# A tile stage written out for 71 tiles, with the routing weight made in the tile from the difference of two logits

## The reference

```python
logits = einsum('bth,he->bte', z, rW) + rb
probs = softmax(logits);  topv, topi = top_k(probs, 2)
mask = sum(one_hot(topi, 8) * topv[..., None], axis=-2)
w = mask / maximum(sum(mask, -1), 1e-8)
hid = gelu(einsum('bth,ehf->btef', z, W1) + b1)          # exact gelu, W1: 8 x 256 x 512
outs = einsum('btef,efh->bteh', hid, W2) + b2            # W2: 8 x 512 x 256
mixed = sum(outs * w[..., None], axis=2);  return x + mixed
```

## Time and profile before

| | |
|---|---|
| median of 3 runs | 596.23 us (595.38 to 596.32) |
| the profiled execution | 598.88 us, of which its span (first to last instruction) 597.0 us |
| granted TensorE clock, mean | 0.937 of full speed |
| busy: PE, PEld, DVE, ACT, POOL | 477.8, 395.3, 443.5, 350.3, 338.7 us |
| tile stage, first hb to last hb | 285.30 to 551.68 us |
| DMA | 69.95 MB in 50125 packets, 10160 of them under 512 B |

### The profile page before, as it was taken

How to read it: one execution, slowest core, us unless ns; L and a number is a source line. 1 busy time by engine, 2 the same in 40 slices (tenths; PEclk the granted TensorE clock), 3 DMA queues, 4 the chain that set the end, 5 groups by cost and what they waited for, 6 DMA issues and landing times.

```text
span 597.0 us, 13147 instructions
## 1 busy us (share of the span) xinstructions
PE 477.8 (80%) x2775; PEld 395.3 (66%) x2776; DVE 443.5 (74%) x1469; ACT 350.3 (59%) x788; POOL 338.7 (57%) x266
## 2 busy tenths in 40 slices
PE   0388899889999885795999999999999999999300
PEld 0138888777888773542797788798887888887200
DVE  6999786999889848347677777777767777777283
ACT  6992845475676567613465565565655565565365
POOL 0000567643778874660367667767666676666547
PEclk9998999989999986988999999999999999999855
DMA  6205700131335669724435444444444443443497
GB/s 183 101 1 205 289 1 1 59 137 47 131 126 168 199 199 326 238 100 126 152 66 79 67 67 72 71 70 71 64 68 71 71 68 65 70 64 51 61 402 284
DMA packets 50125, 69.95 MB, mean 117 GB/s; under 512 B 10160, under 2 KB 39728, under 8 KB 49584
## 3 DMA queue, kind: packets, MB, share of 16 engines
q1 hardware_dynamic: 34528, 51.81, 26.2%
q0 software_dynamic: 15568, 17.81, 17.9%
HBM read 37.90 MB, written 31.69 MB: 117 GB/s over the span
## 4 chain that ended last, share of the span: by engine, by line
PE 45%; DVE 21%; issue 11%; ACT 10%; POOL 5%; DMA 3%; SPq 3%; another core or an unknown queue 1%; POOLq 0%; DVEq 0%; ACTq 0%
PE psum L1436 14%; PE psum L1455 13%; PE psum L1445 5%; PE psum L1330 3%; PE psum L1423 3%; POOL acc L1254 3%; DVE st L702 2%; PE psum L1301 2%; DVE ws L896 2%; SPq L394 1%; PE psum L1288 1%; DMA y_rows<-yw,dst 1%; POOL y_rows L1231 1%; ACT dump L593 1%; PE psum L1350 1%
## 5 line engine op out<-in xcount | busy, mean ns | idle before, releaser
L1231 POOL DMA_INDIRECT y_rows<-yw,dst x71 | 115.7, 1630 | 66.1 <-issue 22.8
L1436 PE MATMUL psum<-ws,z_hl 128*128 x426 | 119.0, 415 | 3.4 <-DVE z_hl L1094 2.5
L1455 PE MATMUL psum<-ws,h_hl 128*128 x852 | 115.9, 285 | 0.1
L1455 PEld LDWEIGHTS psum<-ws,h_hl 128*128 128x128 f32 x852 | 103.5, 189 | 0.3 <-issue 0.3
L1218 POOL DMA_INDIRECT wt<-w_rows,widx x71 | 70.1, 987 | 44.1 <-issue 18.0
L652 ACT ACTIVATE hg<-hb 128x512 f32<-128x512 f32 x71 | 44.9, 632 | 85.1 <-DVE hb L1102 74.6
L1436 PEld LDWEIGHTS psum<-ws,z_hl 128*128 128x128 f32 x426 | 76.3, 190 | 20.3 <-issue 5.2
L1176 POOL DMA_INDIRECT z_rows<-zn,pos x64 | 68.9, 1076 | 27.2 <-issue 17.1
L1102 DVE TENSOR_TENSOR hb<-psum,b1r 128x512 f32<-128x512 f32 x71 | 49.1, 692 | 36.8 <-issue 34.5
L1330 PE MATMUL psum<-yf,it 128*128 128x256 f32 x256 | 60.9, 395 | 2.6 <-DVE r L945 2.6
L638 ACT ACTIVATE z_f<-psum,gb 128x128 f32<-128x128 f32 x142 | 56.0, 443 | 11.1 <-PE psum L1423 8.9
(11 more groups left out here) (206 smaller groups left out, 854.7 us busy)
## 6 DMA issues: line engine op xcount, KB each, us to landing
z_in<-z_rows SPq DMA_DIRECT2D x71, 129.0 KB
w_raw<-in_dram SPq DMA_DIRECT2D x16, 512.0 KB, 5.9
xs<-in_dram SPq DMA_DIRECT2D x8, 512.0 KB, 5.8
x_dram<-xs SPq DMA_DIRECT2D x8, 512.0 KB
y_rows<-zn SPq DMA_DIRECT2D x8, 512.0 KB, 3.3
yr<-y_rows SPq DMA_DIRECT2D x8, 512.0 KB, 6.7
out_dram<-acc SPq DMA_DIRECT2D x7, 512.0 KB, 4.5
b1r<-in_dram SPq DMA_DIRECT2D x8, 256.0 KB
```

The source lines that it names most:

```text
L1231: pool.indirect_dma_start(y_rows, bass.IndirectOffsetOnAxis(ap=dst[m][:, 0:1], axis=0), yw[m % 3][:, :], None, compute_op=ALU.add).then_in ...
L1436: last = TE.matmul(ps_h[q], z_hl[q][:, a, k], w_at(e1, c, k * F, F), start=n == 0, stop=n == 5)
L1455: last = TE.matmul(ps_y[q], h_hl[q][:, a, k], w_at(e2, c, 1024 + k * H, H), start=n == 0, stop=n == 11)
```

## The change

- Each line of `z_rows` gets a third extra column, the difference of its two best logits (`place`, one more DVE instruction per row; W = 259).
- The block that made all weights (L1047 to L1062 on DVE, L625 and L626 on ACT), the store of `w_rows` and the 71 gathers of `wt` on POOL go. With the gathers go DVE's waits for them.
- In the tile, DVE's third small instruction makes `half` = (second expert ? -0.5 : +0.5) times the difference, written as (flag + 0.5) * difference with flag -1 or 0. It takes the place of `widx`. ACT makes `lean` = tanh(half), placed behind z_f, and `wt` = 0.5 + 0.5 * lean one part later, placed between the gelu and yw.
- The loops of all five engines are written out: t is a Python number everywhere, and the tile stage has no branch.

```diff
-W = H + 2
+W = H + 3
-    def tiles(eng, part, peel=0):
+    def tiles(eng, part):
         loaded[eng.engine.name] = {}
-        for i in range(-2, 3 + UNROLL * peel):
-            part(i, i % 2, i)
-        with eng.Fori(peel, (TILES - 5) // UNROLL) as j:
-            loaded[eng.engine.name] = {}
-            for u in range(UNROLL):
-                part(j * UNROLL + (3 + u), (1 + u) % 2, u)
-        loaded[eng.engine.name] = {}
-        for i in range(TILES - 2, TILES + 1):
+        for i in range(-2, TILES + 1):
             part(i, i % 2, i)
@@ SP
-            sp.wait_ge(sem("wgt_ready"), 1)
-            sp.dma_start(w_rows.rearrange("(c p n) o -> p c (n o)", c=2, p=P),
-                         wgt[:, 0:2].rearrange("p c b k -> p c (b k)")).then_inc(sem("w_stored"), 16)
-            load_z(6, 0)
-            load_z(7, 1)
-            release(1, 1)
-            with sp.Fori(3, (TILES - 3) // 2) as j:
-                ...
+            for t in range(6, TILES):
+                load_z(t, t % 2)
+                if t > 6:
+                    release(t - 6, t % 2)
+            for t in range(TILES - 6, TILES):
                 release(t, t % 2)
@@ ACT
-            nc.scalar.activation(wsm[:, :, :, :], wsm[:, :, :, :], ACT.Exp).then_inc(sem("wsm_exp"), 1)
-            nc.scalar.activation(dump[:, 0, 0:1], eps[:, 0:1], ACT.Gelu)
+            nc.scalar.activation(wt[5][:, :], eps[:, 0:1], ACT.Gelu)
             def part(i, par, u):
                     ...  z_f
+                    m = slot(t, u, 2)
+                    act.wait_ge(sem("dest_ready"), t + 1)
+                    nc.scalar.activation(lean[m % 3][:, :], half[m % 3][:, :], ACT.Tanh).then_inc(sem("lean_set"), 1)
                     ...  h_high
                     nc.scalar.activation(hg[q][:, :], hb[:, :], ACT.Gelu).then_inc(sem("hg_ready"), 1)
+                    m = slot(t, u, 1)
+                    act.wait_ge(sem("lean_set"), t + 1)
+                    nc.scalar.activation(wt[m][:, :], lean[m % 3][:, :], ACT.Identity, bias=one_half[:, 0:1],
+                                         scale=0.5).then_inc(sem("wt_set"), 1)
                     act.wait_ge(sem("y_ready"), t + 1)
                     gate(act)
-                    act.wait_ge(sem(f"w_in{q}"), (t - q) * 8 + 16)
+                    act.wait_ge(sem("wt_set"), t + 1)
@@ DVE, front
                 V.tensor_copy(zn[buf(row.b)][:, :, H + 1], mif[:, 1])
+                V.tensor_tensor(zn[buf(row.b)][:, :, H + 2], mx_all[:, row.b, :, 0], mx_all[:, row.b, :, 1], ALU.subtract)
@@ DVE, between the stages: L1047 to L1062 taken out
@@ DVE, tile
-                    V.tensor_scalar(flag[:, :], z_in[q][:, H + 1:W], tab_e[:, bass.ds(t, 1)], float(B * T),
+                    V.tensor_scalar(flag[:, :], z_in[q][:, H + 1:H + 2], tab_e[:, bass.ds(t, 1)], -1.0,
                                     ALU.is_equal, ALU.mult).then_inc(sem("flag_set"), 1)
                     dve.wait_ge(sem("flag_set"), t + 1)
-                    if not early(t, 3):
-                        dve.wait_ge(sem(f"w_in{1 - q}"), (t - 2 + q) * 8)
-                    gate(dve)
-                    V.tensor_tensor(widx[slot(t, u, 2) % 3][:, :], z_in[q][:, H:H + 1], flag[:, :],
-                                    ALU.add).then_inc(sem("dest_ready"), 1)
+                    V.scalar_tensor_tensor(half[slot(t, u, 2) % 3][:, :], flag[:, :], 0.5, z_in[q][:, H + 2:W], ALU.add,
+                                           ALU.mult).then_inc(sem("dest_ready"), 1)
@@ POOL
-            pool.wait_ge(sem("w_stored"), 16)
-            for t in range(4):
-                gather_w(t, t % 2, t % 6)
             ...
-            for t in range(7):
-                gather_w(t + 4, t % 2, (t + 4) % 6)
-                scatter_y(t, t % 2, t % 6)
-            with pool.Fori(1, (TILES - 5) // UNROLL) as j:
-                ...
-            for t in range(TILES - 4, TILES):
+            for t in range(TILES):
                 scatter_y(t, t % 2, t % 6)
```

More of the change, by code:

```diff
@@ L84, in program @@
     kf = at("kf", [P, 2, KT, H], F32, 104 * KB)
-    zn = [at(f"zn{i}", [P, 4, W], F32, 120 * KB + 4 * i * 4 * W) for i in range(2)]
+    zn = [at(f"zn{i}", [P, 4, W], F32, 120 * KB + 4160 * i) for i in range(2)]
     zn += [at("zn2", [P, 4, W], F32, 64 * KB)]
-    zn += [at(f"zn{i}", [P, 4, W], F32, o0 + 4 * (i - 3) * 4 * W) for i in (3, 4, 5)]
+    zn += [at(f"zn{i}", [P, 4, W], F32, o0 + 64 + 4160 * (i - 3)) for i in (3, 4, 5)]
     xn = [at(f"xn{i}", [P, 4, H], F32, k) for i, k in enumerate((o0, 120 * KB, 124 * KB))]
@@ L153, in program @@
     order = at("order", [1, TILES + 1], I32, o0 + 71 * KB + 736)
-    widx = [at(f"widx{i}", [P, 1], U32, o0 + 71 * KB + 32 * i) for i in range(3)]
+    half = [at(f"half{i}", [P, 1], F32, o0 + 71 * KB + 32 * i) for i in range(3)]
+    lean = [at(f"lean{i}", [P, 1], F32, o0 + 71 * KB + 96 + 32 * i) for i in range(3)]
     wt = [at(f"wt{i}", [P, 1], F32, o0 + 50 * KB + 768 + 32 * i) for i in range(6)]
+    one_half = at("one_half", [P, 1], F32, c0 + 6624)
     yw = [at(f"yw{i}", [P, H], F32, o0 + k * KB) for i, k in enumerate((69, 70, 49))]
@@ L301, in live @@
     def live(t):
-        return not isinstance(t, int) or 0 <= t < TILES
+        return 0 <= t < TILES
     def expert(eng, t, u):
@@ L310, in slot @@
     def slot(t, u, ahead):
-        return (t if isinstance(t, int) else u + 3 + ahead) % UNROLL
+        return t % 6
     def early(t, n=1):
-        return isinstance(t, int) and t < n
+        return t < n
     with nc.Block() as block:
@@ L400, in load_z @@
                 row = sp.value_load(tab[0:1, 0, bass.ds(t, 1)], min_val=0, max_val=ROWS - P)
-                if not (isinstance(t, int) and t < 2):
+                if t >= 2:
                     sp.wait_ge(sem("tz_mm"), t - 1)
@@ L426, in _ @@
             sp.wait_ge(sem("order_ready"), 1)
-            load_z(6, 0)
-            load_z(7, 1)
-            release(1, 1)
-            with sp.Fori(3, (TILES - 3) // 2) as j:
-                load_z(j * 2 + 2, 0)
-                release(j * 2 - 4, 0)
-                load_z(j * 2 + 3, 1)
-                release(j * 2 - 3, 1)
-            load_z(TILES - 1, 0)
-            for t in range(TILES - 7, TILES):
+            for t in range(6, TILES):
[3 more added lines that the diff above has]
+            for t in range(TILES - 6, TILES):
                 release(t, t % 2)
@@ L661, in part @@
                     nc.scalar.activation(yw[m % 3][:, :], y_sb[q][:, :], ACT.Identity, scale=wt[m][:, 0:1]).then_inc(sem("yw_ready"), 1)
-            tiles(act, part, 1)
+            tiles(act, part)
             part(TILES + 1, (TILES + 1) % 2, TILES + 1)
@@ L737, in _ @@
             V.memset(eps[:, 1:2], EPS * EPS)
+            V.memset(one_half[:, :], 0.5)
             V.memset(rnd[:, :], ROUND).then_inc(sem("one"), 1)
@@ L1208, in _ @@
             steps(step)
-            def gather_w(t, q, m):
-                if not early(t, 2):
-                    pool.wait_ge(sem(f"w_in{q}"), (t - q) * 8)
-                    gate(pool)
-                pool.wait_ge(sem("dest_ready"), t + 1)
-                gate(pool)
-                pool.indirect_dma_start(wt[m][:, 0:1], None, w_rows,
-                                        bass.IndirectOffsetOnAxis(ap=widx[m % 3][:, 0:1], axis=0)).then_inc(sem(f"w_in{q}"), 16)
             def scatter_y(t, q, m):
@@ L1239, in _ @@
             pool.wait_ge(sem("trash_set"), 32)
-            for t in range(7):
-                gather_w(t + 4, t % 2, (t + 4) % 6)
-                scatter_y(t, t % 2, t % 6)
-            with pool.Fori(1, (TILES - 5) // UNROLL) as j:
-                for u in range(UNROLL):
-                    gather_w(j * UNROLL + (5 + u), (1 + u) % 2, (5 + u) % 6)
-                    scatter_y(j * UNROLL + (1 + u), (1 + u) % 2, (1 + u) % 6)
-            for t in range(TILES - 4, TILES):
+            for t in range(TILES):
                 scatter_y(t, t % 2, t % 6)
```

23 lines of the change are left out of this document (1 added, 22 removed).

## The result

The changed kernel takes 600.26 us (median of 20 runs, 595.79 to 603.92) against 596.48 for the kernel before (20 runs): the ratio is 1.0061, 95% interval 1.0034 to 1.0088. So it is slower by 0.6%, about 3.6 us. The forecast was 597.7, range 589.5 to 603.5, with "slower" as the likeliest. The profiled execution took 603.01 us, its span is 601.2.

A forecast was written before the change was run, and what follows sets the result against it. A ring between ACT and DVE, slightly slower than PE, was taken as the bound. Stage +1.4 us, between stages -0.1 and front +0.2 made +1.5: 600.4 profiled, less 2.65 for the median, 597.7; range 589.5 to 603.5.

The forecast's parts named there:

- The register work: DVE ahead of hb: with t a number, idle falls from 0.50 to 0.41; 0.10 less a tile, -6.6 us.
- wt, +0.19: ACT between gelu and yw: wt adds 0.19 us to each of 69 steps, +13.1 us (bounds +6.9 and +14.5).
- Rival B: ACT between gelu and yw: wt costs only the 0.10 of a copy, giving 591.5 us; chance 0.20.
- lean in a shade: ACT behind z_f, where it then idles 1.5 us: lean costs 0; without that idle 0.1 to 0.4 a tile.
- PE's pauses: PE at its loop's turns: 11 pauses, 12.5 us in all, go, but the ring doesn't wait for PE: 0.
- PE needs 3.5 us a tile: Tile stage: PE's matmuls, from 238.7 us busy over 67.5 tiles; six tiles with one pause take 22.2 us.
- the ring: Tile stage: ACT and DVE wait on each other from hb to hb, 3.73 to 3.75 us a tile, slower than PE.
- a sign of being wrong: Gelu-to-yw step not growing, or PE without idle time and hb waiting for L1436, would refute the prediction.
- The gathers go: POOL: 71 gathers leave; four of five long steps of 4.7 to 5.0 us were to go with them, -4.4 us.
- rival C: Written-out code starves a sequencer: DVE pays 1.2 us at some six fetches, +7, giving 604.7 us; chance 0.10.
- Front and end: Front: eight small DVE instructions, +0.2 us (0 to 0.6). End: last scatters wait for landings, not POOL, 0.
- rival E: ACT swaps tables between tanh and gelu: two loads of 1.28 us, 71 times, +182 us, giving 780; chance 0.02.

The follow-up runs named there:

- the loops alone: Kernel before with its tile loops written out, table and gathers kept: 585.25 us, ratio 0.9892.
- wt twice: Changed kernel with a second instruction of wt's kind behind the first, between gelu and yw, into a spare column: 611.27 us, ratio 1.0341.
- the read moved: Kernel before, loops written out, with DVE's read of the next tile's expert moved to the start of the tile's part; table and gathers kept: ratio 0.9637.
- the table's traffic: Changed kernel with the weight store and 71 gathers put back, into tiles that nothing reads: ratio 1.0049.
- wt in the shade: Changed kernel with wt moved from between gelu and yw to right behind lean, where ACT idles anyway: 585.61 us, ratio 0.9907.
- the fastest: Changed kernel with DVE's read of the next tile's expert moved to the start of the tile's part, wt left in place: 573.75 us, ratio 0.9593.

## Why the prediction was right, and where it wasn't

**The register work, -0.10.** Right: 3.64 with the loops alone, and "issue" 0.41 for 0.50.

**wt, +0.19.** Right: 0.18 in the timeline, 0.18 as the difference between 3.82 and 3.64, nothing when moved into ACT's idle time, 0.18 when doubled. The instruction takes 278 ns, near the 297 of the row it was read from the earlier trace rows, and yw starts 0.10 before it ends. Rival B, the likeliest of the rivals, is out. The step is 3.82 where I wrote 3.83.

**lean in a shade, 0.** Right. In wt's experiment even both small instructions fit there.

**PE's pauses, 0.** Right, and shown by writing out PE alone. But the reading "PE needs 3.5 us a tile", taken from its busy time, was not sound, though it came near the 3.45 of PE's beat once PE sets the pace. The window's 1584 matmuls are 66 tiles at 24 each, not 67.5, since it holds long steps; by the same busy time that makes 3.62 a tile, and six of them with one pause 22.9 us, more than the ring's 22.5. The busy time went up to 250.87 of 253 at 3.82 a tile with PE not the bound, to 199.31 of 200 at 3.64, and it is 200 of 200 where PE is the bound. PE idle in small pieces, which I had wanted to see in every tile, shows only as the weight load's wait for the gelu. PE had next to no idle time, half of what I had named as a sign of being wrong; the other half, hb waiting for L1436, didn't come: hb waits for "issue" in 68 tiles. The busy time of PE includes its short waits; its count of matmuls in a stretch doesn't.

**The gathers go, -4.4.** This is the step that failed; that its number came near is luck. The five long steps went, 5.7 us over the normal in the earlier trace rows's profile, and not four of them, and 1.4 us of new stops came. I had argued from four rows out of five that a gather makes the stop. The runs show an interaction. Counting long steps with the read of the expert in its old place: rolled with gathers 5, 5, 2 and, with PE written out, 2; rolled without gathers 0; written out with gathers 0 and 0; written out without 0 (but for wt twice, whose usual step is already 4.00). So at this pace the gathers' going gave nothing that writing out the loops hadn't given already. With the read moved, the written-out kernel with gathers has 4, so they are harmless only beside a slower ring. A coincidence in one column of a profile was taken for the cause. What a gather and a loop's turn do to each other isn't shown.

**Straight code, rival C.** It exists, at a fifth of the size. Steps longer by 0.35 come at the same tiles (32, 47, 62) in four written-out kernels (changed, in both profiles; with the table's traffic; wt in the shade; wt twice), always with 0.74 to 0.76 of "issue" before hb. The kernel before, written out, has four such steps at other tiles (21, 30, 37, 44), and the rolled kernel with the formula one, at tile 7. The two queues that carry instructions moved 27 and 36 packets in the changed kernel; in the kernel before, run again, 11 and 18:

```profile
q8 instruction: 11, 0.18, 0.1%
q14 instruction: 18, 0.15, 0.1%
```

With PE alone written out they are 27 and 18, so the packets of q8 come with PE's code. Four such steps are 1.4 us, not the 7 of six full pauses. That they are fetches is my reading of place and spacing; no row joins a packet to a step.

So the stage came out as 3 x 3.42 + 66 x 3.82 + 1.4 = 263.8, measured 263.7, forecast 265.4: the difference is 0.7 for the step's 0.01 and 0.9 for stops that were expected to stay.

**Front and end.** +0.2 and 0 were forecast; the end took 1.0 more, and the front by my reading 1 to 2. By two profiles each the changed kernel's stage is 263.5 against 263.2, so the 3.6 us of the medians lie for the larger part outside the stage. I had the sign of the whole from a stage that in fact came out even, which is luck too. In the profile the miss (603.01 against a forecast of 600.4) is 3.3 us in front of the stage (half of it because the routing began at 96.80 instead of 95.08, which is chance) and 1.1 behind it, less the 1.7 by which the stage was shorter than forecast.

**Tables and straight code.** The Trainium skill's page "ScalarE: Activation LUTs", section on table sets, was weighed as rival E. The trace decides against it here: one load for the stage (L607, 1283 ns), then 71 times tanh, gelu, identity and copy in turn without another. Of the Trainium skill's page "Runtime: NRT & Kernel Launch", section on instruction fetch, the trace agrees that the pauses of a loop's turn go (PE's 12.5 us). That straight code streams without a stop it wouldn't bear out if the steps of 4.17 are fetches, which no row shows.

**Why slower.** By the times, writing out the loops gave 1.1% and the formula took 1.7%, some 10 us. By the stages the two nearly cancel: the loops gave 10 to 12 us (register work, turns and long steps together), and one instruction of 0.18 us, put 69 times into the one stretch of ACT that has no gap, took 12.4 by the ring (263.5 less 252.2 is 11.3). What is left over, some 3 us, lies in front of the stage and behind it.

## What to carry to other kernels

Where two engines hand work back and forth with no slack, add up the starts around the ring before placing anything: a tiny instruction costs its full 0.18 us a round between gelu and yw and nothing where the engine idles anyway, and a register read that nobody counts as work was worth 0.4 us a round, 3.6% of the kernel together with the written-out loops. When the ring falls under the next bound, the same tiny instruction becomes free: shorten the ring first, then judge what stands in it. And a cause that is read from events standing side by side in one profile should be tried from both sides, since here each of the two suspects alone was harmless at the pace that the kernel had.

## What the runs showed of the hardware

- ACT instructions on 128x1 take 193 ns (tanh) and 278 ns (wt) by the profile, but cost the engine's stream 0.09 and 0.18 to 0.19 us; tanh ran from the table that was loaded for gelu.
- PE's busy time doesn't tell whether PE is the bound. 200 us of the stage hold 1252 matmuls at 198.5 us busy in the changed kernel and 1393 at 200.0 in the fastest, at the same mean of 415 and 416 ns for the matmuls of the first layer. Nor does PE's share of the chain: 45 and 55% in two profiles of the kernel before, 55% in the fastest. The even beat of 3.44 and 3.46 us a tile without a wait does.
- The steps of the ring repeat within 0.01 us from run to run, while the same program's front moves by 3 us and its long steps change place and size.
- With the table's store and gathers gone, the last entry of the chain begins 7.0 us before the end of the span instead of 6.0, in seven profiles against six; putting that traffic back, unused, restores 6.0. The cause is open.
